# Cross attention scores: the low-key products of two neighbouring tiles as two 64-row products in the two halves of the array

## The chip, the cores and the metric

The kernel runs on one core of one Trainium2 chip. A core has TensorE (PE) for matmuls, VectorE (DVE), ScalarE (ACT) and GpSimd (POOL) for the rest, and SyncE (SP), which here issues the DMAs. Each engine takes its instructions in order and waits on semaphores. The metric is the device time of one execution in microseconds (us). Before the change three runs took 3082.76, 3084.55 and 3085.52 us; the median is 3084.55.

## The reference

A perceiver-like network of 6 layers on 4 batches, then a small attention and a gated recurrence over the batches. Per layer and batch: causal self attention over 128 rows, cross attention of 128 rows over a context of 2048 rows, and a gated feed-forward part. All are 16 heads of width 64 with one key/value head that the heads share. What the change touches is the score product of the cross attention:

```python
q = (xn @ wq).reshape(b, n, H, DH).transpose(0, 2, 1, 3) * SCALE      # 16 heads x 128 rows
k, v = jnp.split(kv @ wkv, 2, axis=-1)                                # kv is the context, 2048 rows
nk, nv = null_kv                                                      # one more key and value
k = jnp.concatenate((nk, k), axis=1)
q = l2norm(q) * math.sqrt(SCALE)
k = l2norm(k) * math.sqrt(SCALE)
sim = jnp.einsum('bhid,bjd->bhij', q, k)
attn = jax.nn.softmax(sim, axis=-1)
out = jnp.einsum('bhij,bjd->bhid', attn, v)
```

## The kernel before

**Precision.** Queries and keys are each split into a high and a low fp16 half of width 64 (high = the fp16 rounding, low = the rest). `QT[:, par]` holds the turned queries: high in partitions 0 to 63, low in 64 to 127, 2048 columns (16 heads x 128 rows). `KT[:, par, part]` holds the turned keys twice: part 0 is high over low, part 1 low over high. A tile's score is two full 128-row matmuls, part 0 and part 1, into one PSUM bank (`scores`, line 936), which gives all four products of halves. The probabilities are split too: `PH` is the rounded exponential, `P` the full one (both ACT, lines 786 and 789), `PL = P - PH` (DVE, line 549), and the value product is three matmuls, V with PH, VL with PH and V with PL (lines 985, 986, 988).

**Rounds and steps.** There are 24 runs (6 layers x 4 batches). Each has 64 tiles (4 groups of 4 heads x 16 tiles of 128 keys). The function `drive` writes, for every engine, windows of 65 steps. In a window the tiles ("core") of run n stand beside the front of run n+1 (self attention, projections, keys and queries of the cross attention) and the back of run n-1 (output, feed-forward). Step 0 is the scores of the null key, step s from 1 the tile s-1. After the core's step come the stages that a table names for this step: PLAN_PE, PLAN_ACT, PLAN_DVE and PLAN_POOL. An engine never leaves this order. Names with f_ belong to the front, with b_ to the back, with e_ to the core.

**A step of PE.** Scores of tile s-1 into bank `s % 3` of psS, and the value sums of the tile of step s-AHEAD (AHEAD = 6). Before it writes the bank, step s waits until ACT has finished with the tile of step s-3, `pe.wait_ge(sem("ca_exp"), n * TILES + s - SLOTS)`. ACT takes a step's two exponentials, then its stages; DVE in step s takes the subtraction of step s-1. P has 4 slots, PH and PL 8.

**Stages that matter here.** On PE: f_proj_sa (step 5) projects the self attention's queries; f_turn_q_sa (15) turns them; f_sk1 (25) gives self attention scores, which ACT's f_se1 (23 of ACT's table) takes; f_sv1 and b_up stand at 31, f_sk2 at 32, f_sk3 at 37, f_sv3 at 43, f_wo at 48; f_proj_ca and f_turn_k0 at 53, f_turn_k1 at 56, f_turn_q_ca at 62. f_turn_k0 and f_turn_k1 turn the keys, 16 transposes each, which ACT (line 868) and DVE (line 610) copy into KT. ACT's f_QT_ca (line 804) copies the queries into QT, after which the next round's step 0 may begin.

Of the kernel before, what the change touches and what calls it, by code (L numbers as in the profile page):

```python
# [36 lines left out]
AHEAD = 6  # L37
# [25 lines left out]
def build(nc, x, ctxT, wpack, gcols, gout, null_k, null_v, tail_w, tail_cols, bo, emb,  # L63
          c_pack, out):
    with ExitStack() as ctx:
# [89 lines left out]
        ks = sb("ks", [128, KT_N, 3, DH], F16)  # L155
        KT = sb("KT", [128, 2, 2, M], F16)
# [23 lines left out]
        PL = sb("PL", [128, HSLOTS, QCOL], F32R)  # L180
# [43 lines left out]
        def at(s, core, back):  # L224
# [17 lines left out]
            31: ["f_se2"], 36: ["f_se3"], 52: ["f_raw_ca"], 53: ["f_KT0", "f_sq_ca"], 56: ["f_KT1"], 58: ["f_hi_ca"],  # L242
# [40 lines left out]
        def _(sp):  # L283
# [37 lines left out]

            for n in range(1, B):
                context(n)
            with sp.Fori(1, L) as l:
                context(l * B)
                sp.wait_ge(sem("ca_proj"), l * B * 2)
                front_weights(l)
                context(l * B + 1)
                sp.wait_ge(sem("ff_w2"), l * B)
                back_weights(l)  # L330
                context(l * B + 2)
                context(l * B + 3)
            sp.wait_ge(sem("ca_proj"), RUNS * 2)
# [9 lines left out]
        def _(pool):  # L343
# [40 lines left out]
            def low(tag, half, whole, high):  # L384
# [10 lines left out]
                "f_klow": low("kv", ks[:, :, 1, :], kn[:], ks[:, :, 0, :]),  # L395
# [13 lines left out]
        def _(dve):  # L409
# [130 lines left out]
            def core_step(s, core, back):  # L540

                step = at(s - LOW, core, back)
                if step is None or step[0] == 0:
                    return
                t, n, par = step[0] - 1, step[1], step[2]
                dve.wait_ge(sem("p_hi"), n * TILES + t + 1)
                dve.wait_ge(sem("ca_exp"), n * TILES + t + 1)
                here = t % HSLOTS
                nc_v.tensor_tensor(PL[:, here, :], P[:, t % PSLOTS, :], PH[:, here, :], ALU.subtract).then_inc(sem("p_lo"), 1)  # L549
# [210 lines left out]
        def _(act):  # L760
# [98 lines left out]
            def f_khi(n, par):  # L859
                act.wait_ge(sem("kv_kn"), n + 1)  # L860
                for a in (0, 2):
# [3 lines left out]
            def f_KT(part):  # L865
                def stage(n, par):
                    act.wait_ge(sem("kv_T"), n * 4 + 2 * part + 1)
                    nc_a.activation(KT[:, par, part, 0:1024], psLh[0].rearrange("p t c -> p (t c)"), ACT.Copy).then_inc(sem("kv_KT_a"), 1)
                return stage
# [13 lines left out]
            for part in range(2):  # L883
                stages[f"f_KT{part}"] = f_KT(part)
# [23 lines left out]
        def _(pe):  # L908
# [40 lines left out]
            def core_step(s, core, back):  # L949

                if core is not None:
                    n, par = core
                    first = isinstance(n, int) and n == 0
                    if s == 0:
                        pe.wait_ge(sem("ca_QT"), n * 2 + 2)
                        pe.wait_ge(sem("kv_KT_a"), n * 2 + 2)
# [4 lines left out]
                    if s == SLOTS:  # L961
                        pe.wait_ge(sem("ca_nexp"), n + 1)
                    elif s > SLOTS:
                        pe.wait_ge(sem("ca_exp"), n * TILES + s - SLOTS)
                    elif not first:
                        pe.wait_ge(sem("ca_exp"), n * TILES - (STEPS - 1 - max(t for t in range(STEPS - SLOTS, STEPS) if t % SLOTS == s)))
                    bank = psS[:, s % SLOTS, :]
                    if s == 0:
                        null_scores(bank, [nkc[:, par, p, :] for p in range(2)], QT[:, par], True).then_inc(sem("ca_nqk"), 1)
                    else:  # L970
                        g, j = (s - 1) // KT_N, (s - 1) % KT_N
                        scores(bank, [KT[:, par, p, 128 * j:128 * j + 128] for p in range(2)], QT[:, par, g * QCOL:(g + 1) * QCOL]).then_inc(sem("ca_qk"), 1)
# [15 lines left out]
                mm(bank, V[:, par, j, :], PL[:, here, :], start=False, stop=(j == KT_N - 1)).then_inc(sem("ca_pv"), 1)  # L988
# [81 lines left out]
            def f_turn_q_ca(n, par):  # L1070
                pe.wait_ge(sem("kv_KT_a"), n * 2 + 2)
# [3 lines left out]
            def f_turn_k(part):  # L1075
                def stage(n, par):
                    pe.wait_ge(sem("kv_lo"), n + 1)
                    for i in range(2):
                        if part == 1:
                            pe.wait_ge(sem("kv_KT_a" if i == 0 else "kv_KT_v"), n * 2 + 1)  # L1080
                        else:
                            pe.wait_ge(sem("ca_raw"), n * 2 + i + 1)
                        for t in range(8):
                            ins = nc.tensor.transpose(psLh[i][:, t, :], ks[:, 8 * i + t, part:part + 2, :].rearrange("p a d -> p (a d)"), ident16[:])
                        ins.then_inc(sem("kv_T"), 1)
                return stage
# [33 lines left out]
            for part in range(2):  # L1120
                stages[f"f_turn_k{part}"] = f_turn_k(part)
# [138 lines left out]
```

## Time and profile before

| | |
|---|---|
| median of 3 runs | 3084.55 us |
| profiled execution: its own time / its span | 3083.15 us / 3081.4 us |
| PE busy (matmuls) | 2670.2 us, 87% of the span |
| DVE busy | 2352.4 us, 76% |
| ACT busy | 2115.6 us, 69% |
| POOL busy | 606.1 us, 20% |
| mean granted TensorE clock | 0.944 of full speed |
| scores of the tiles (line 939) | 3072 matmuls |
| value sums (lines 985, 986, 988) | 1536 matmuls each |

The span is from the first to the last instruction. Matmuls overlap, and each one's duration in the profile is its way through the array; how fast PE really goes is read from start to start. An engine's idle time is put down to the engine and line that ended it last.

### The profile page before, as it was taken

The numbers are of one execution on the slowest core, as the hardware profiler recorded it, in microseconds if no ns is written. First come the engines' busy times: TensorE is split into PE (matmuls) and PEld (weight loads), VectorE is DVE, ScalarE is ACT, GpSimd is POOL, SyncE is SP. The second block draws the span as 40 slices with busy tenths as digits, with TensorE's granted clock in tenths as the row PEclk, the third lists the DMA queues.
The fourth block names the chain that finished last, engine by engine and source line by source line (L and its number), as shares of the span: only waits on it lengthen the run. The fifth ranks groups of instructions, "written<-read, shape, count | busy, mean of one in ns | idle before, by whom it ended". The sixth has DMA issues, their size and how long they took to land.

```text
span 3081.4 us, 44915 instructions
## 1 busy us (share of the span) xinstructions
PE 2670.2 (87%) x13036; PEld 1575.0 (51%) x13036; DVE 2352.4 (76%) x4396; ACT 2115.6 (69%) x3898; POOL 606.1 (20%) x392
## 2 busy tenths in 40 slices
PE   3698988998998988989989999898899989989856
PEld 1355545555554555555555555555455555555535
DVE  4587877877777877877788787787778778787665
ACT  2487777777777767768678677777777777677601
POOL 2212212212212213113113023022122122120000
PEclk8799999999999999999999999999999999999866
DMA  3000000000000000001001001001001001000000
GB/s 109 14 1 15 15 24 15 1 32 16 15 24 15 1 32 15 1 14 38 1 1 47 1 14 38 1 1 47 1 14 39 1 1 47 1 1 12 1 1 4
DMA packets 11436, 51.72 MB, mean 17 GB/s; under 512 B 1361, under 2 KB 6018, under 8 KB 6410
## 3 DMA queue, kind: packets, MB, share of 16 engines
q1 hardware_dynamic: 11146, 48.28, 4.5%
q8 instruction: 129, 2.11, 0.3%
q14 instruction: 161, 1.32, 0.1%
HBM read 47.99 MB, written 0.29 MB: 16 GB/s over the span
## 4 chain that ended last, share of the span: by engine, by line
PE 49%; DVE 18%; issue 16%; ACT 10%; POOL 5%; DVEq 1%; DMA 0%; ACTq 0%; SPq 0%; POOLq 0%
PE psS L939 13%; PE psO L985 7%; PE psO L986 6%; PE psO L988 6%; ACT P L789 5%; DVE PL L549 5%; ACT PH L786 3%; POOL rn L353 3%; PE psL L1031 3%; PE psL L939 2%; PE psL L1042 2%; PE psL L1049 1%; DVE rows_sb L528 1%; PE psL L1032 1%; DVE oTs L533 1%
## 5 line engine op out<-in xcount | busy, mean ns | idle before, releaser
L549 DVE TENSOR_TENSOR PL<-P,PH 128x512 fp32r<-128x512 f32 x1536 | 1168.1, 785 | 129.4 <-ACT P L789 83.6
L786 ACT ACTIVATE PH<-psS 128x512 fp32r<-128x512 f32 x1536 | 944.5, 615 | 250.8 <-PE psS L939 227.2
L939 PE MATMUL psS<-QT,KT 128*128 128x512 f16 x3072 | 949.8, 393 | 14.8 <-ACT P L789 12.4
L789 ACT ACTIVATE P<-psS 128x512 f32<-128x512 f32 x1536 | 949.7, 618 | 18.8 <-DVE PL L549 16.2
L985 PE MATMUL psO<-PH,V 128*128 128x512 f32 x1536 | 902.8, 588 | 0.0
L986 PE MATMUL psO<-PH,VL 128*64 128x512 f32 x1536 | 614.9, 400 | 0.0
L988 PE MATMUL psO<-PL,V 128*128 128x512 f32 x1536 | 613.7, 400 | 0.0
L985 PEld LDWEIGHTS psO<-PH,V 128*128 128x128 f32 x1536 | 299.7, 195 | 208.3 <-issue 33.7
L939 PEld LDWEIGHTS psS<-QT,KT 128*128 128x128 f16 x3072 | 219.0, 100 | 354.0 <-issue 232.3
L988 PEld LDWEIGHTS psO<-PL,V 128*128 128x128 f32 x1536 | 295.0, 192 | 152.3 <-issue 8.1
L353 POOL TENSOR_TENSOR front_rstd<-front_ve,neghalf 128x1 f32<-128x1 f32 x84 | 45.5, 542 | 1491.9 <-DVE front_ve L417 1491.9
L353 POOL TENSOR_TENSOR rn<-ssc,neghalf 128x16 f32<-128x16 f32 (+2 forms) x73 | 235.0, 3220 | 359.8 <-DVE ssc L484 306.2
L837 ACT ACTIVATE Ps<-psL 128x512 f32<-128x512 f32 x96 | 57.7, 601 | 288.1 <-PE psL L939 288.1
L986 PEld LDWEIGHTS psO<-PH,VL 128*64 128x64 f32 x1536 | 215.3, 140 | 40.4
L939 PE MATMUL psL<-QTs,KTs 128*128 128x512 f16 x192 | 67.9, 441 | 101.4 <-DVE oTs L533 99.2
L388 POOL TENSOR_TENSOR qs_all<-qsq,qs_all 128x1088 f16<-128x1088 f32 (+1 forms) x48 | 116.4, 2426 | 139.3 <-ACT qs_all L796 139.3
L528 DVE STREAM_TRANSPOSE rows_sb<-rcol 64x512 f32<-64x512 f32 x192 | 135.8, 707 | 5.2
L932 PE MATMUL psL<-ident,qs_all 128*128 128x128 f16 x768 | 55.8, 230 | 87.2 <-POOL qs_all L388 61.0
L578 DVE TENSOR_TENSOR Ps<-Ps,ET 128x512 f32<-128x512 f32 x96 | 66.0, 688 | 73.1 <-ACT Ps L837 73.1
L808 ACT ACTIVATE qraw<-psL 128x512 f32<-128x512 f32 x96 | 57.3, 597 | 82.7 <-PE psL L1049 62.2
L1061 PEld LDWEIGHTS psL<-W,ctx_sb 128*128 128x128 f32 x768 | 99.0, 192 | 26.0 <-ACT qraw L808 14.4
L1061 PE MATMUL psL<-W,ctx_sb 128*128 128x128 f32 x768 | 104.0, 279 | 3.5 <-ACT kraw L851 3.5
(310 smaller groups left out, 2947.7 us busy)
## 6 DMA issues: line engine op xcount, KB each, us to landing
ctx_sb<-ctxT SPq DMA_DIRECT2D x24, 1024.0 KB, 4.8
W<-wpack SPq DMA_DIRECT2D x6, 1664.0 KB, 6.3
W<-wpack SPq DMA_DIRECT2D x6, 1280.0 KB, 5.6
ctx_sb<-biasM SPq DMA_DIRECT2D x1, 1024.0 KB
W<-tail_w SPq DMA_DIRECT2D x1, 832.0 KB
kraw<-biasW SPq DMA_DIRECT2D x1, 512.0 KB
ksq<-biasW SPq DMA_DIRECT2D x1, 512.0 KB
P<-null_v SPq DMA_DIRECT2D x1, 384.0 KB
```

The source lines that it names most:

```text
L353: nc.gpsimd.tensor_tensor(out_, in_, neghalf[0:out_.shape[0], 0:width], ALU.pow).then_inc(sem(done), 1)
L388: nc.gpsimd.tensor_tensor(half, whole, high, ALU.subtract).then_inc(sem(tag + "_lo"), 1)
L528: nc_v.transpose(rr, rc.unsqueeze(2).broadcast_to([64, QCOL // 32, 32])).then_inc(sem(tag + "_row"), 1)
L549: nc_v.tensor_tensor(PL[:, here, :], P[:, t % PSLOTS, :], PH[:, here, :], ALU.subtract).then_inc(sem("p_lo"), 1)
L786: nc_a.activation(PH[:, t % HSLOTS, :], bank, ACT.Exp, scale=SIM_SCALE).then_inc(sem("p_hi"), 1)
L789: nc_a.activation(P[:, t % PSLOTS, :], bank, ACT.Exp, scale=SIM_SCALE).then_inc(sem("ca_exp"), 1)
L939: ins = mm(bank, keys[part], q, start=(part == 0), stop=(part == 1))
L985: mm(bank, V[:, par, j, :], PH[:, here, :], start=False, stop=False)
L986: mm(bank[0:DH, :], VL[:, par, j, :], PH[:, here, :], start=False, stop=False)
L988: mm(bank, V[:, par, j, :], PL[:, here, :], start=False, stop=(j == KT_N - 1)).then_inc(sem("ca_pv"), 1)
L1031: mm(psL[:, g % 2, :], Vs[:], Ps[:, g % 2, :], start=True, stop=False)
L1061: ins = mm(psL[:, t % 2, a * 128:(a + 1) * 128], ctx_sb[:, k * 128:(k + 1) * 128], weights(W_CAKV, W_CAKV + 128), start=True, stop=True)
```

## The change

The scores of a tile become one full product and one half product. KT now holds the high keys twice, so that one full matmul gives high keys times high and low queries. The low keys stand in KL: those of even tiles in partitions 0 to 63, those of odd tiles in 64 to 127, and are multiplied with the high queries only. For odd tiles the high queries must stand in partitions 64 to 127 too; SP copies them there by a DMA of 64 x 2048 fp16 values (QB). At an odd step PE issues the half products of this tile and of the next, into two banks, and then this tile's full product; at an even step only the full product. The product of low keys and low queries is no longer computed. Keys now need 24 transposes instead of 32, and one ACT copy less. PL shrinks from 8 to 4 slots, with a wait of DVE for the value sum of the tile four back, and AHEAD goes from 6 to 5.

```diff
-AHEAD = 6
+LSLOTS = 4
+AHEAD = 5
...
-        ks = sb("ks", [128, KT_N, 3, DH], F16)
-        KT = sb("KT", [128, 2, 2, M], F16)
+        ks = sb("ks", [128, KT_N, 2, DH], F16)
+        kl = sb("kl", [128, KT_N // 2, 2, DH], F16)
+        KT = sb("KT", [128, 2, M], F16)
+        KL = sb("KL", [128, 2, M // 2], F16)
+        QB = sb("QB", [128, 2, H * N], F16)
...
-            31: ["f_se2"], 36: ["f_se3"], 52: ["f_raw_ca"], 53: ["f_KT0", "f_sq_ca"], 56: ["f_KT1"], 58: ["f_hi_ca"],
+            31: ["f_se2"], 36: ["f_se3"], 52: ["f_raw_ca"], 53: ["f_KT0", "f_sq_ca"], 58: ["f_hi_ca"],
...
+            def queries_below(n, par):
+                sp.wait_ge(sem("ca_QT"), n * 2 + 2)
+                sp.dma_start(QB[64:128, par, :], QT[0:64, par, :]).then_inc(sem("ca_QB"), 16)
...
+                if t >= LSLOTS or not isinstance(n, int) or n > 0:
+                    dve.wait_ge(sem("ca_pv"), n * TILES + t - LSLOTS + 1)
+                nc_v.tensor_tensor(PL[:, t % LSLOTS, :], P[:, t % PSLOTS, :], PH[:, here, :], ALU.subtract).then_inc(sem("p_lo"), 1)
...
-                    dve.wait_ge(sem("kv_T"), n * 4 + 2 * part + 2)
-                    ins = nc_v.tensor_copy(KT[:, par, part, 1024:2048], psLh[1].rearrange("p t c -> p (t c)"))
-                    ins.then_inc(sem("kv_KT_v"), 1)
+                    dve.wait_ge(sem("kv_T"), n * 3 + 2 + part)
+                    dst = KL[:, par, :] if part else KT[:, par, 1024:2048]
+                    nc_v.tensor_copy(dst, psLh[1 - part].rearrange("p t c -> p (t c)")).then_inc(sem("kv_KT_v"), 1)
...
-                    elif s > SLOTS:
-                        pe.wait_ge(sem("ca_exp"), n * TILES + s - SLOTS)
...
-                        scores(bank, [KT[:, par, p, 128 * j:128 * j + 128] for p in range(2)], QT[:, par, g * QCOL:(g + 1) * QCOL]).then_inc(sem("ca_qk"), 1)
+                        t = s - 1
+                        g, j = t // KT_N, t % KT_N
+                        cols = slice(g * QCOL, (g + 1) * QCOL)
+                        if t % 2 == 0:
+                            if s == 1:
+                                pe.wait_ge(sem("ca_QB"), n * 16 + 16)
+                            if s == SLOTS:
+                                pe.wait_ge(sem("ca_nexp"), n + 1)
+                            if s >= SLOTS or not first:
+                                pe.wait_ge(sem("ca_exp"), n * TILES + max(0, s + 1 - SLOTS))
+                            pair = slice(64 * j, 64 * j + 128)
+                            mm(bank, KL[0:64, par, pair], QT[0:64, par, cols], start=True, stop=False)
+                            mm(psS[:, (s + 1) % SLOTS, :], KL[64:128, par, pair], QB[64:128, par, cols], start=True, stop=False)
+                        mm(bank, KT[:, par, 128 * j:128 * j + 128], QT[:, par, cols], start=False, stop=True).then_inc(sem("ca_qk"), 1)
...
+            def f_turn_k1(n, par):
+                pe.wait_ge(sem("kv_KT_a"), n + 1)
+                for t in range(8):
+                    ins = nc.tensor.transpose(psLh[0][:, t, :], kl[:, t].rearrange("p a d -> p (a d)"), ident16[:])
+                ins.then_inc(sem("kv_T"), 1)
```

The order on PE at steps 25 and 26, before. The names are output<-inputs, ca_exp counts the tiles that ACT is done with, psL<-QTs,KTs is the self attention score f_sk1:

```order
L939 MATMUL psS<-QT,KT 128x512 [waits ca_exp]
L939 MATMUL psS<-QT,KT 128x512
L985 MATMUL psO<-PH,V 128x512 [waits p_hi]
L986 MATMUL psO<-PH,VL 64x512
L988 MATMUL psO<-PL,V 128x512 [waits p_lo]
L939 MATMUL psL<-QTs,KTs 128x512 [waits sa_nexp,sa_KT,sa_QT]
L939 MATMUL psL<-QTs,KTs 128x512
L964 REGISTER_ALU
L939 MATMUL psS<-QT,KT 128x512 [waits ca_exp]
```

The same place of the changed kernel:

```order
L992 MATMUL psS<-QT,KL 128x512 [waits ca_exp]
L993 MATMUL psS<-QB,KL 128x512
L994 MATMUL psS<-QT,KT 128x512
L1006 REGISTER_ALU
L1007 MATMUL psO<-PH,V 128x512 [waits p_hi]
L1008 MATMUL psO<-PH,VL 64x512
L1010 MATMUL psO<-PL,V 128x512 [waits p_lo]
L953 MATMUL psL<-QTs,KTs 128x512 [waits sa_nexp,sa_KT,sa_QT]
L953 MATMUL psL<-QTs,KTs 128x512
L994 MATMUL psS<-QT,KT 128x512
```

The odd step now has three score matmuls, two of them with 64 rows, and carries the only wait for ca_exp of the pair; the even step has one matmul and no such wait.

The DMA issues of SP in the loop over layers, before (ISA and REGISTER_ALU rows only compute addresses and counts):

```order
L320 DMA ctx_sb<-ctxT 128x2048 [waits kv_proj]
L326 REGISTER_ALU
L290 ISA [waits ca_proj]
L290 DMA W<-wpack 128x3328
L291 ISA
L291 DMA gsa<-gout 128x128
L319 ISA
L320 DMA ctx_sb<-ctxT 128x2048 [waits kv_proj]
```

And changed:

```order
L324 DMA ctx_sb<-ctxT 128x2048 [waits kv_proj]
L336 REGISTER_ALU
L294 ISA [waits ca_proj]
L294 DMA W<-wpack 128x3328
L295 ISA
L295 DMA gsa<-gout 128x128
L328 ISA
L329 DMA QB<-QT 64x2048 [waits ca_QT]
L323 ISA
L324 DMA ctx_sb<-ctxT 128x2048 [waits kv_proj]
```

The copy QB stands behind the context of the next run and, once in four runs, behind the weights of the next layer, in SP's one queue; the following context stands behind QB.

## Rows read from the trace of the kernel before

**Rows 1.** Page, section 1 and section 5: busy time by engine; a group of instructions.
```profile
PE 2670.2 (87%) x13036; PEld 1575.0 (51%) x13036; DVE 2352.4 (76%) x4396; ACT 2115.6 (69%) x3898; POOL 606.1 (20%) x392
...
L549 DVE TENSOR_TENSOR PL<-P,PH 128x512 fp32r<-128x512 f32 x1536 | 1168.1, 785 | 129.4 <-ACT P L789 83.6
```
**Rows 2.** Timeline of PE, a bare step: start us, us, engine, line, operation.
```profile
1528.18 0.61 PE L939 MATMUL psS<-QT,KT 128*128 128x512 f16 x2
...
1529.10 0.39 PE L988 MATMUL psO<-PL,V 128*128 128x512 f32 x1
1529.33 0.60 PE L939 MATMUL psS<-QT,KT 128*128 128x512 f16 x2
```
**Rows 3.** Timeline of PE around matmuls of another shape (rows*columns of the array).
```profile
1564.51 0.39 PE L988 MATMUL psO<-PL,V 128*128 128x512 f32 x1
1564.83 0.62 PE L946 MATMUL psL<-QTs,nkcs 128*32 128x512 f16 x8
1565.38 0.49 PE L1025 MATMUL psL<-B,group_rows 8*128 8x512 f32 x1
1565.80 0.60 PE L939 MATMUL psS<-QT,KT 128*128 128x512 f16 x2
```
**Rows 4.** Timeline of PE: scores of step 25, f_sk1, scores of step 27.
```profile
1570.28 0.60 PE L939 MATMUL psS<-QT,KT 128*128 128x512 f16 x2
...
1571.42 0.60 PE L939 MATMUL psL<-QTs,KTs 128*128 128x512 f16 x2
...
1573.69 0.60 PE L939 MATMUL psS<-QT,KT 128*128 128x512 f16 x2 [0.54 <-ACT P L789]
```
**Rows 5.** Timeline of ACT: P of step 23, f_se1, P of steps 24 and 25.
```profile
1570.32 0.61 ACT L789 ACTIVATE P<-psS 128x512 f32<-128x512 f32 x1
1572.06 0.60 ACT L837 ACTIVATE Ps<-psL 128x512 f32<-128x512 f32 x1 [1.13 <-PE psL L939]
...
1573.03 0.60 ACT L789 ACTIVATE P<-psS 128x512 f32<-128x512 f32 x1
...
1573.98 0.63 ACT L789 ACTIVATE P<-psS 128x512 f32<-128x512 f32 x1
```
**Rows 6.** Timelines of PE and ACT: scores of step 39, P of step 37.
```profile
1599.63 0.60 PE L939 MATMUL psS<-QT,KT 128*128 128x512 f16 x2
...
1599.67 0.60 ACT L789 ACTIVATE P<-psS 128x512 f32<-128x512 f32 x1
```
**Rows 7.** Waits of the whole execution: us in total, times, longest us.
```profile
PE psL L939 <- DVE oTs L533: 99.2, 22, 4.5
PE psL L932 <- POOL qs_all L388: 61.0, 25, 7.9
...
PE psS L939 <- ACT P L789: 12.4, 23, 0.5
...
DVE hu L629 <- PE psA L1097: 108.3, 24, 4.7
```
**Rows 8.** Timelines of PE and ACT at a round's end: transposes, QT, null scores, step 1.
```profile
1521.70 1.05 PE L932 MATMUL psL<-ident,qs_all 128*128 128x128 f16 x16 [1.14 <-DVE KT L610]
...
1522.72 1.94 ACT L804 ACTIVATE QT<-psL 128x1024 f16<-128x1024 f16 x2
...
1525.69 0.61 PE L946 MATMUL psS<-QT,nkc 128*32 128x512 f16 x8 [0.66 <-ACT P L789]
...
1527.03 0.61 PE L939 MATMUL psS<-QT,KT 128*128 128x512 f16 x2
```
**Rows 9.** Timeline of ACT: the second key copy and the high query halves.
```profile
1513.44 1.13 ACT L868 ACTIVATE KT<-psL 128x1024 f16<-128x1024 f16 x1
...
1517.17 1.06 ACT L796 ACTIVATE qs_all<-qsq 128x1024 f16<-128x1024 f32 x1 [0.64 <-DVE qsq L491]
```
**Rows 10.** DMA issues: how many, KB each, median us from issue to landing.
```profile
ctx_sb<-ctxT SPq DMA_DIRECT2D x24, 1024.0 KB, 4.8
...
out<-x_in SPq DMA_DIRECT2D x4, 64.0 KB, 1.5
```

More of the change, by code:

```diff
@@ L179, in build @@
         PH = sb("PH", [128, HSLOTS, QCOL], F32R)
[L180 removed]
+        PL = sb("PL", [128, LSLOTS, QCOL], F32R)
         Pn = sb("Pn", [128, QCOL], F32R)
@@ L860, in f_khi, with f_KT0 @@
                 act.wait_ge(sem("kv_kn"), n + 1)
-                for a in (0, 2):
+                for a in range(2):
                     ins = nc_a.activation(ks[:, :, a, :], kn[:], ACT.Copy)
                 ins.then_inc(sem("kv_hi"), 1)
[L865 to L869, printed above, removed]
+            def f_KT0(n, par):
+                act.wait_ge(sem("kv_T"), n * 3 + 1)
+                nc_a.activation(KT[:, par, 0:1024], psLh[0].rearrange("p t c -> p (t c)"), ACT.Copy).then_inc(sem("kv_KT_a"), 1)
             def b_tanh(n, par):
@@ L882, in _ @@
                 stages[f"f_kraw{g}"] = f_kraw(g)
-            for part in range(2):
-                stages[f"f_KT{part}"] = f_KT(part)
+            stages["f_KT0"] = f_KT0
             drive(act, PLAN_ACT, stages, core_step)
@@ L959, in core_step @@
                         pe.wait_ge(sem("kv_v"), n * 4 + 4)
-                    if s == SLOTS:
-                        pe.wait_ge(sem("ca_nexp"), n + 1)
-                    elif s > SLOTS:
-                        pe.wait_ge(sem("ca_exp"), n * TILES + s - SLOTS)
-                    elif not first:
-                        pe.wait_ge(sem("ca_exp"), n * TILES - (STEPS - 1 - max(t for t in range(STEPS - SLOTS, STEPS) if t % SLOTS == s)))
                     bank = psS[:, s % SLOTS, :]
                     if s == 0:
+                        if not first:
+                            pe.wait_ge(sem("ca_exp"), n * TILES - 1)
                         null_scores(bank, [nkc[:, par, p, :] for p in range(2)], QT[:, par], True).then_inc(sem("ca_nqk"), 1)
                     else:
-                        g, j = (s - 1) // KT_N, (s - 1) % KT_N
-                        scores(bank, [KT[:, par, p, 128 * j:128 * j + 128] for p in range(2)], QT[:, par, g * QCOL:(g + 1) * QCOL]).then_inc(sem("ca_qk"), 1)
+                        t = s - 1
[12 more added lines that the diff above has]
+                        mm(bank, KT[:, par, 128 * j:128 * j + 128], QT[:, par, cols], start=False, stop=True).then_inc(sem("ca_qk"), 1)
                 step = at(s - AHEAD, core, back)
@@ L987, in core_step @@
                 pe.wait_ge(sem("p_lo"), n * TILES + t + 1)
-                mm(bank, V[:, par, j, :], PL[:, here, :], start=False, stop=(j == KT_N - 1)).then_inc(sem("ca_pv"), 1)
+                mm(bank, V[:, par, j, :], PL[:, t % LSLOTS, :], start=False, stop=(j == KT_N - 1)).then_inc(sem("ca_pv"), 1)
             def weights(a, b):
@@ L1070, in f_turn_q_ca, with f_turn_k0 @@
             def f_turn_q_ca(n, par):
-                pe.wait_ge(sem("kv_KT_a"), n * 2 + 2)
+                pe.wait_ge(sem("kv_KT_a"), n + 1)
                 pe.wait_ge(sem("kv_KT_v"), n * 2 + 2)
                 turn_q("ca")(n, par)
[L1075 to L1086, printed above, removed]
+            def f_turn_k0(n, par):
+                pe.wait_ge(sem("kv_lo"), n + 1)
+                for i in range(2):
+                    pe.wait_ge(sem("ca_raw"), n * 2 + i + 1)
+                    for t in range(8):
+                        ins = nc.tensor.transpose(psLh[i][:, t, :], ks[:, 8 * i + t].rearrange("p a d -> p (a d)"), ident16[:])
+                    ins.then_inc(sem("kv_T"), 1)
+            def f_turn_k1(n, par):
+                pe.wait_ge(sem("kv_KT_a"), n + 1)
+                for t in range(8):
+                    ins = nc.tensor.transpose(psLh[0][:, t, :], kl[:, t].rearrange("p a d -> p (a d)"), ident16[:])
+                ins.then_inc(sem("kv_T"), 1)
             def b_gate(n, par):
@@ L1119, in _ @@
                 stages[f"f_kv{g}"] = f_kv(g)
-            for part in range(2):
-                stages[f"f_turn_k{part}"] = f_turn_k(part)
+            stages["f_turn_k0"], stages["f_turn_k1"] = f_turn_k0, f_turn_k1
             drive(pe, PLAN_PE, stages, core_step)
```

10 lines of the change are left out of this document (7 added, 3 removed).

## The prediction

> **What bounds the kernel now.** I read the page first: PE is busy 87% of the span, ACT 69%, DVE 76% [rows 1]. One profiled execution took 3083.15 us, of which the span is 3081.4; the median of the runs is 1.4 us above it. The work repeats in rounds of about 117.8 us, one per batch and layer: 64 score tiles in 64 steps, and between them the stages of the next round's front and the last one's back. 24 rounds have tiles, 23 of them beside a front. I number steps as the code does, step 0 being the null scores.
>
> The timeline of PE shows a bare step: from one pair of score matmuls to the next 1.15 us, for five passes of 512 columns, so 0.23 each [rows 2]. ACT, when it has a backlog, needs 0.95 us for a tile's two exponentials (from 1573.03 to 1573.98 in [rows 5]). So in bare steps PE is the limit and ACT has 0.2 us to spare, out of which it must pay its front stages (0.6 to 2 us each) in clumps.
>
> The waits show where neither counts. PE waits for the query halves at step 15 (POOL's qs_all, 61.0 us in 25 times), at step 32 for the scaled self attention (oTs, 99.2 us in 22 times, up to 4.5), both in [rows 7], and at step 62 for the key copy (1.14 us in [rows 8]). These end chains over ACT, POOL and DVE that a PE stage started: the projection at step 5, the "up" product at step 31 (DVE itself waited 108.3 us for it), the second value product at step 43, the cross projection at step 53. Whatever PE saves between the start and the end of such a chain becomes a longer wait. The end of the round is one chain from step 53 to step 0: after the transposes (step 62) comes QT on ACT, then two tiles, and only then do the null scores start [rows 8].
>
> **The score passes.** Before, two full matmuls for each tile; now an odd step has two half-array ones, meant to run side by side (one pass), and a full one, an even step one full one. Free of other cost that saves one pass of 0.23 us in each even step. But the array changes its shape before and after the halves. The nearest rows: a full matmul to the 32-column null scores took 0.32 us instead of 0.23; the eight of these took 0.55 to the next, two passes (0.46) and 0.09; and the 8-row matmul to the next full one 0.42, which is 0.19 above a pass, with an exposed fp32 weight load in it [rows 3]. So a change of shape costs 0.09 to 0.19 us; I take 0.09, the two f16 cases, since KL, KT and nkc are all f16. Odd step: 1.15 + 2 x 0.09 = 1.33, that is +0.18. Even step: 1.15 - 0.23 = 0.92, that is -0.23. A pair gains 0.05 us, and since chains start at odd steps (5, 25, 31, 37, 43, 53), a stretch often has one odd step more.
> The Trainium skill, "TensorEngine Tiling (Array Packing)", Key Properties, says that changing the tiling mode drains the array, which speaks against this change; [rows 3] agree with 0.09. By its table Theoretical Speedup alone (up to 2x for 64 rows) the whole pass would be gained; that is the first rival below. That two row halves start within some 4 ns is in "TensorE: Matmul & The Clock Gate", The mechanism; no row here shows row halves, the four column groups of [rows 3] behave so.
>
> **The tighter wait, the main term.** Step s used to wait for the exponentials of step s-3. An odd step now opens two banks at once and waits for step s-2; an even step waits for none. Queued behind this wait are all of PE's matmuls of the step and the stages after it. Where ACT works off a clump this is late:
> - Step 25: PE began it at 1570.28 [rows 4]; the exponentials of step 23 ended at 1570.32 + 0.61 = 1570.93 [rows 5]. Late by 0.65.
> - Step 27: began at 1573.69 after 0.54 of waiting for step 24 [rows 4]; step 25's end at 1573.98 + 0.63 = 1574.61, late by 0.92. It doesn't merge with the first: between them ACT waited 1.13 us for the self attention score that PE issues behind step 25 [rows 5], so both add.
> - Step 39: began at 1599.63, step 37's end at 1600.27: late by 0.64 [rows 6].
> - Elsewhere (steps 7 and 61) it is late too, but inside the chains 5 to 15 and 53 to 0, which have the room; at other odd steps it is early by 0.5 and more in bare stretches.
>
> **Smaller parts.** (a) QB: 256 KB moved by DMA once QT is done. QT ends at 1522.72 + 1.94 = 1524.66, step 1 begins at 1527.03 [rows 8], so 2.4 us are free. 64 KB landed in 1.5 us, 1024 KB in 4.8 [rows 10]; a line through both gives 2.2 for 256 KB. I take 0.1 us of stall; bounds nothing and 2.4 us (4.8 less 2.4) a round. SP issues it behind a context load and weights that were released long before step 62. (b) Eight transposes and one ACT copy of 1.1 us fewer per round. The copy stood at 1513.44, and ACT then waited anyway until 1517.17 for DVE's unit queries [rows 9]: nothing gained. The transposes go inside the same chain: nothing. If both lay on the path: 1.1 + 0.5 us a round. (c) PL has 4 slots, so DVE waits for the sum four tiles back; with the sums one step earlier (AHEAD 5) that sum is issued in the same step, where DVE comes later than PE in nearly all steps: nothing, bound 0.8 us a round (the mean length of one such DVE operation [rows 1]). The last sums end one step earlier: -1 us once. The low-times-low product that is dropped costs and saves nothing by itself.
>
> **The sum for a round.** Steps 1 to 5: 3 x 0.18 - 2 x 0.23 = +0.1, with QB +0.2. Steps 5 to 15: hidden. Steps 16 to 22, until ACT's clump begins: 3 x 0.18 - 4 x 0.23 = -0.4. Step 25: +0.65 - 0.35 = +0.3. Step 27: + 0.09 + 0.92 = +1.3. To step 31: +0.0. The chain to step 32 keeps its length. Steps 33 to 37 +0.1, step 39 +0.6. 39 to 43: 0. 43 to 48 hidden. 49 to 53: +0.1. 53 to 0 hidden. In all 0.2 + 1.3 + 0.7 + 0.1 = 2.3 us. Times 23: +53. The last round has no front: 32 pairs x -0.05 = -1.6. With the -1 at the end: +50. 3083.15 + 50 + 1.4 = **3135 us** by the median.
>
> **Rivals.**
> 1. The change of shape is hidden (halves are loaded while the array drains). Odd steps +0, even -0.23: stretch 1 to 5 -0.4, the clump at 25 is met early, 27 leaves +0.5, 33 to 39 +0.2, 39 to 43 -0.5, 49 to 53 -0.5: -0.6 a round, -14 us, 3070; with the transposes and the copy on the path too (1.6 x 23 = 37) 3034. For: nothing in [rows 3]. It decides below about 0.04 us a change. Chance 0.21, faster.
> 2. The waits at 25, 27 and 39 don't add up to 2.2 but to the one at 27, since ACT starts its clump earlier: 2.3 - 1.3 - 0.6 = +0.4, less the transposes: within 0.2%, 3086. Chance 0.10.
> 3. The halves run one after the other. Each of about 16 odd steps outside the chains pays 0.23 more: 3.7 x 23 = +85, 3220. Against: the column groups of [rows 3] overlap. Likewise with changes of 0.19 (0.2 more in as many): 3205. Chance 0.14.
> 4. QB lands 2.4 us late in each round: +55, 3190. Chance 0.06.
> The forecast has 0.49. Results within 0.2% (6 us) can't be told from no change. Faster 0.21 (rival 1), same 0.10, slower 0.69. The range from 3060 to 3215 leaves out the far end of rivals 1 and 3; the forecast's own is 3105 to 3170.
>
> **What would show it.** In the changed profile: the half matmuls of a pair start within 0.01 us of each other, and the full one 0.3 us later, not 0.23; bare pairs take 2.25 us, not 2.30. PE's waits for ACT's P before the scores, 12.4 us in all before [rows 7], come to 50 or more, in groups at steps 25, 27 and 39, while the waits for qs_all and oTs grow a little. DMA QB lands in 2 to 2.5 us and PE hardly waits for it. ACT's busy time falls by some 26 us (24 copies), to no effect. It is wrong if a bare pair takes 2.1 us or less, or if a round comes out at or below 117.8 us.

## The result, and the profile after

The changed kernel takes 3185.2 us (median of 4 runs, 3183.88 to 3188.49), the kernel before beside it 3085.0. The ratio is 1.0328, 95% interval 1.0310 to 1.0346: slower by 100 us. The prediction said slower by 50. The time lies inside its whole range (3060 to 3215), but outside the 3105 to 3170 that it gave for its own mechanism.

The profiled execution of the changed kernel took 3188.49 us, its span 3186.7. Busy time by engine, and the group of the subtraction P - PH on DVE, against [rows 1]:

```profile
PE 2686.3 (84%) x12844; PEld 1495.6 (47%) x12844; DVE 2341.8 (73%) x4396; ACT 2075.3 (65%) x3874; POOL 611.3 (19%) x392
...
L566 DVE TENSOR_TENSOR PL<-P,PH 128x512 fp32r<-128x512 f32 x1536 | 1156.7, 774 | 267.9 <-PE psO L1010 218.1
```

ACT has 40 us less work, and PE 192 instructions fewer (with 16 us more busy time, since some of them run at the lower clock), and both only idle more. The bare steps came out nearly as forecast. Timeline of PE after (start us, us, engine, line), one pair of bare steps, against [rows 2]:

```profile
1684.67 0.39 PE L992 MATMUL psS<-QT,KL 64*128 64x512 f16 x1
1684.68 0.39 PE L993 MATMUL psS<-QB,KL 64*128 64x512 f16 x1
1685.00 0.39 PE L994 MATMUL psS<-QT,KT 128*128 128x512 f16 x1
...
1685.92 0.39 PE L994 MATMUL psS<-QT,KT 128*128 128x512 f16 x1
...
1686.62 0.39 PE L1010 MATMUL psO<-PL,V 128*128 128x512 f32 x1
1686.94 0.39 PE L992 MATMUL psS<-QT,KL 64*128 64x512 f16 x1
```

The two halves start 0.01 us apart, the full product 0.32 behind them, and at 1686.94 the next halves 0.32 behind a full one, instead of 0.23: two changes of shape of 0.09 each. The pair takes 2.27 us (1684.67 to 1686.94), against two bare steps of 1.15 before, so the two changes of shape eat nearly all of the pass that the halves save. The Trainium skill, "TensorEngine Tiling (Array Packing)", Key Properties, says that a change of the tiling mode drains the array; the trace agrees, with 0.09 us for each.

The waits of the whole execution (us in total, times, longest), against [rows 7]:

```profile
PE psS L992 <- ACT P L806: 110.2, 78, 2.0
PE psL L953 <- DVE oTs L548: 103.7, 22, 4.7
PE psL L946 <- POOL qs_all L403: 55.9, 25, 9.4
...
PE psO L1010 <- DVE PL L566: 13.5, 22, 0.6
...
PE psS L992 <- DMA QB<-QT: 9.5, 15, 1.9
```

The first was 12.4 us before and has grown most. The timelines of one round show steps 25 and 27, against [rows 4, 5]. PE:

```profile
1621.22 0.40 PE L1010 MATMUL psO<-PL,V 128*128 128x512 f32 x1
1622.37 0.39 PE L992 MATMUL psS<-QT,KL 64*128 64x512 f16 x1 [0.76 <-ACT P L806]
...
1624.74 0.39 PE L1010 MATMUL psO<-PL,V 128*128 128x512 f32 x1
1626.86 0.39 PE L992 MATMUL psS<-QT,KL 64*128 64x512 f16 x1 [1.73 <-ACT P L806]
```

ACT at the same time:

```profile
1621.71 0.60 ACT L806 ACTIVATE P<-psS 128x512 f32<-128x512 f32 x1
1624.25 0.60 ACT L854 ACTIVATE Ps<-psL 128x512 f32<-128x512 f32 x1 [1.94 <-PE psL L953]
...
1626.18 0.63 ACT L806 ACTIVATE P<-psS 128x512 f32<-128x512 f32 x1
```

Step 25 starts when P of step 23 is done (1621.71 + 0.60), 0.76 late, and step 27 when P of step 25 is done (1626.18 + 0.63), 1.73 late where it was 0.54 before. Between the two ACT waits 1.94 us for the self attention scores that PE issues behind step 25: the waits do add up. Step 39, against [rows 6]:

```profile
1653.29 0.50 PE L1005 MATMUL psO<-Pn,nv 32*128 32x512 f32 x1
...
1654.29 0.40 PE L1010 MATMUL psO<-PL,V 128*128 128x512 f32 x1
1654.82 0.39 PE L992 MATMUL psS<-QT,KL 64*128 64x512 f16 x1
```

Here the gap is 1654.82 less 1654.29, 0.53, of which 0.32 is usual: 0.2 late, not 0.64. With AHEAD 5 the null value's matmul (L1005), one step earlier than before, stands in step 38 and fills the rest.

The end of the round went otherwise than forecast. Timelines at steps 60 to 62, against [rows 8, 9]. PE:

```profile
1688.88 0.39 PE L1010 MATMUL psO<-PL,V 128*128 128x512 f32 x1
1691.28 0.39 PE L992 MATMUL psS<-QT,KL 64*128 64x512 f16 x1 [2.01 <-ACT P L806]
...
1692.53 0.60 PE L994 MATMUL psS<-QT,KT 128*128 128x512 f16 x1
...
1693.35 0.63 PE L1008 MATMUL psO<-PH,VL 128*64 128x512 f32 x1
1693.78 0.63 PE L1010 MATMUL psO<-PL,V 128*128 128x512 f32 x1
1694.21 1.93 PE L946 MATMUL psL<-ident,qs_all 128*128 128x128 f16 x16
```

ACT there:

```profile
1689.20 1.06 ACT L813 ACTIVATE qs_all<-qsq 128x1024 f16<-128x1024 f32 x1 [1.68 <-DVE qsq L506]
...
1690.64 0.59 ACT L806 ACTIVATE P<-psS 128x512 f32<-128x512 f32 x1
1691.12 0.60 ACT L803 ACTIVATE PH<-psS 128x512 fp32r<-128x512 f32 x1
```

ACT stands in f_hi_ca 1.68 us for DVE, then computes qs_all, and only then P of step 59, for which step 61 now waits: 2.01 us. After that the matmuls start 0.43 apart instead of 0.23 (1693.35 to 1693.78), and the 16 transposes take 1.93 instead of 1.05. The clock tells why. Windows of that place (stretch: length, busy us of PE, PEld, DVE, ACT, POOL, then the granted clock):

```profile
1688.90:1691.20 2.30, 0.38 (x2) 0.00 (x0) 2.17 (x6) 2.00 (x4) 0.87 (x1) 1.00 0.00 0
1691.30:1692.50 1.20, 1.20 (x6) 0.61 (x6) 1.20 (x1) 1.20 (x3) 1.16 (x1) 1.00 0.00 0
1692.60:1695.90 3.30, 3.30 (x21) 2.47 (x20) 3.30 (x6) 2.35 (x5) 0.00 (x0) 0.50 0.02 5
```

PE idled for most of 2.3 us, ran 1.2 us at 2.4 GHz and then 3.3 us at 1.2 GHz. In steps 60 to 64 this happened in 16 of 23 rounds, 54.6 us at the lower level in all, and in none before. The mean clock is 0.934, before it was 0.944.

The lengths by stretch. A round of the tiles takes 117.9 us before and 122.1 after (from a run's first score product to the next run's, mean over rounds 4 to 21, the first being 0), +4.2; the 23 rounds together are 97 us longer. The table has the cumulated difference to the kernel before, in us a round, up to the first score product of a step, and beside it the forecast's own sum. It goes by odd steps: an odd step now holds three of the pair's four score products, so that an even step starts later by construction:

| up to step | 25 | 27 | 31 | 37 | 43 | 53 | 59 | next round |
|---|---|---|---|---|---|---|---|---|
| forecast | +0.5 | +1.5 | +1.5 | +1.6 | +2.2 | +2.3 | +2.3 | +2.3 |
| changed kernel | +1.1 | +2.2 | +2.2 | +2.7 | +2.8 | +2.9 | +2.5 | +4.2 |

### The profile page after: what moved, and what is told of

The parts are those of the page before. It is cut to its first block, busy times and chain, and to the rows that moved or that the text cites. A ratio compares the mean times of both kernels' runs of the same rounds, so it can differ in the third digit from the quotient of the medians.

```text
span 3186.7 us, 44651 instructions
## 1 busy us (share of the span) xinstructions
PE 2686.3 (84%) x12844; PEld 1495.6 (47%) x12844; DVE 2341.8 (73%) x4396; ACT 2075.3 (65%) x3874; POOL 611.3 (19%) x392
## 4 chain that ended last, share of the span: by engine, by line
PE 64%; issue 9%; ACT 9%; DVE 9%; POOL 5%; DMA 2%; DVEq 1%; ACTq 0%; SPq 0%; POOLq 0%
PE psS L994 11%; PE psO L1007 9%; PE psO L1010 9%; PE psO L1008 9%; PE psS L992 7%; POOL rn L368 3%; ACT P L806 3%; PE psL L1053 3%; ACT PH L803 2%; POOL qs_all L403 2%; PE psL L953 2%; PE psL L1064 2%; DMA QB<-QT 1%; PE psL L1071 1%; PE psL L1083 1%
## 5 line engine op out<-in xcount | busy, mean ns | idle before, releaser
L1010 PE MATMUL psO<-PL,V 128*128 128x512 f32 x1536 | 622.2, 405 | 13.5 <-DVE PL L566 13.5
L994 PE MATMUL psS<-QT,KT 128*128 128x512 f16 x1536 | 612.8, 399 | 0.0
L992 PE MATMUL psS<-QT,KL 64*128 64x512 f16 x768 | 305.3, 397 | 122.8 <-ACT P L806 110.2
L1007 PEld LDWEIGHTS psO<-PH,V 128*128 128x128 f32 x1536 | 313.8, 204 | 40.1 <-issue 27.8
L994 PEld LDWEIGHTS psS<-QT,KT 128*128 128x128 f16 x1536 | 149.8, 98 | 341.3 <-issue 333.2
L993 PE MATMUL psS<-QB,KL 64*128 64x512 f16 x768 | 305.3, 397 | 0.0
L992 PEld LDWEIGHTS psS<-QT,KL 64*128 64x128 f16 x768 | 71.3, 93 | 376.6 <-ACT P L806 237.8
```

The costliest lines, as they stand in the source:

```text
L992: mm(bank, KL[0:64, par, pair], QT[0:64, par, cols], start=True, stop=False)
L993: mm(psS[:, (s + 1) % SLOTS, :], KL[64:128, par, pair], QB[64:128, par, cols], start=True, stop=False)
L994: mm(bank, KT[:, par, 128 * j:128 * j + 128], QT[:, par, cols], start=False, stop=True).then_inc(sem("ca_qk"), 1)
L1007: mm(bank, V[:, par, j, :], PH[:, here, :], start=False, stop=False)
L1010: mm(bank, V[:, par, j, :], PL[:, t % LSLOTS, :], start=False, stop=(j == KT_N - 1)).then_inc(sem("ca_pv"), 1)
```

## Experiments

Each was timed beside the kernel before (3081.9, 3083.2, 3085.4 and 3085.0 us in four groups). A difference is to the kernel before of the same group; two kernels of different groups are compared by these differences. "A round" is measured as above. "Half clock" is time at the lower of the two levels of the granted clock, 1.2 GHz instead of 2.4; it is summed over the 23 rounds of the profiled execution.

**1. The wait alone.** The old order of passes, the tighter wait.

```diff
-                        pe.wait_ge(sem("ca_exp"), n * TILES + s - SLOTS)
+                        pe.wait_ge(sem("ca_exp"), n * TILES + s - SLOTS + s % 2)
```

> The kernel before, with one change: odd steps wait for the exponentials of step s-2 instead of s-3. No half products, no QB, AHEAD 6. Theory A (the tighter wait, and the half clock that PE falls into behind the longer waits, are the loss): slower by 60 to 110 us, PE's wait for ACT P before the scores above 80 us in all, a gap of about 2 us at step 61. Rival B (the changes of the array's shape and the longer odd steps are the loss): at most 15 us slower.

3127.5 us, ratio 1.0143 (1.0126 to 1.0160), +46. PE waits 95.2 us in 118 times for P before the scores. Up to step 43 a round is 2.3 us longer, but 0.7 comes back at step 48 (a shorter wait of f_wo), and the 1.4 at step 61 comes back by step 63. The loss lies between what the two theories gave, nearer to A: the wait alone costs nearly half of the 100 us. The gap at step 61 is 1.2 us, not the 2 that A named, and no half clock follows it; in all the rounds have 94 us of half clock, fewer than the 155 before.

**2. Pair order with full products.** The changed kernel's order, its wait, but 128-row low products, no KL, no QB.

```diff
+                        if t % 2 == 0:
+                            ...
+                            for i in range(2):
+                                mm(psS[:, (s + i) % SLOTS, :], KT[:, par, 1, 128 * (j + i):128 * (j + i) + 128], QT[:, par, cols], start=True, stop=False)
+                        mm(bank, KT[:, par, 0, 128 * j:128 * j + 128], QT[:, par, cols], start=False, stop=True).then_inc(sem("ca_qk"), 1)
```

> The kernel before, but an odd step opens both banks with the two low-over-high products as full 128-row matmuls and then its own high-over-low one; an even step has one matmul. Same wait as the changed kernel, no change of shape, no QB, AHEAD 6. A pair of bare steps should take 2.29 us. Theory A: within 15 us of the changed kernel (3170 to 3200). Rival B: clearly faster than that, 3100 or less.

3160.9 us, ratio 1.0253 (1.0236 to 1.0270), +79, again between the theories and near A: most of the loss without a single half product. Over experiment 1 it adds 1.8 us a round, 0.7 of it between steps 31 and 37, where 6.1 us a round instead of 3.8 run at half clock behind the wait for oTs. The rest comes in smaller pieces, most of them after step 53.

**3. PL and AHEAD.** The kernel before with AHEAD 5, 4 slots of PL and DVE's wait; and with AHEAD 5 only.

```diff
-AHEAD = 6
+LSLOTS = 4
+AHEAD = 5
...
+                if t >= LSLOTS or not isinstance(n, int) or n > 0:
+                    dve.wait_ge(sem("ca_pv"), n * TILES + t - LSLOTS + 1)
```

> The kernel before with AHEAD 5, PL in 4 slots and DVE's wait for the value sum four tiles back, nothing else. Both theories, as the prediction had it: within 5 us of before. Rival C (the 218 us for which DVE waits for PE's value sums in the changed kernel delay the stages behind them): slower by 20 us or more.

> The kernel before with AHEAD 5 and nothing else, PL in 8 slots without DVE's wait. Theory A: as slow as with both edits (3115 to 3130). Rival C: within 5 us of before.

Both: 3125.3 us, 1.0142 (1.0126 to 1.0159), +43: rival C of the first holds, and "nothing" was wrong for this part by itself. AHEAD 5 only: 3102.2 us, 1.0065 (1.0048 to 1.0082), +19: here neither theory came true, for AHEAD and the slots have about half each. Timeline of PE at step 19 with both:

```profile
1573.44 0.40 PE L989 MATMUL psO<-PH,VL 128*64 128x512 f32 x1
1574.66 0.50 PE L991 MATMUL psO<-PL,V 128*128 128x512 f32 x1 [0.82 <-DVE PL L552]
```

DVE is behind with its front stages, and with the sum one step earlier PE waits 0.82 us for PL, where it had a step in hand before.

**4. All but the halves.** Experiments 2 and 3 together: the change without KL, QB and the fewer transposes.

> The kernel before with everything of the change except the halves: pair order and its wait with full 128-row low products, AHEAD 5 and 4 PL slots; no KL, no QB, all 32 key transposes and the ACT copy kept. Theory A (the halves are worth 0.04 us in an odd step, and eight transposes fewer 0.5 us a round): 0.6 + 0.5 us a round more than the changed kernel, 3200 to 3215 us. Theory B (the halves save a good part of a pass after all and the change's other parts hide it): 3225 or more. Theory C (the halves cost more than the passes they save, or QB does): at or below 3180.

3160.4 us, ratio 1.0242 (1.0225 to 1.0259), +75. Two findings. AHEAD 5 and PL add nothing to pair order (+79 without them): at step 23 this kernel is 0.7 us a round behind experiment 2, at step 25, behind the wait for P, only 0.1. And the changed kernel is 25 us slower than this one, so the halves, with QB and with fewer transposes and one copy less, did not gain a little but lost, as theory C said.

**5. Where the halves lose: the clock at steps 61 to 64.** Three edits of the changed kernel at the end of the round: eight unused matmuls in PE's wait at step 60; f_hi_ca one step later on ACT; the eight transposes of the low keys twice, so that PE has as many as before.

```diff
-            56: ["f_turn_k1"], 62: ["f_turn_q_ca"],
+            56: ["f_turn_k1"], 60: ["f_warm"], 62: ["f_turn_q_ca"],
...
+                for _ in range(8):
+                    mm(psL[:, 1, :], QTs[:, 0:128], QTs[:, 0:512], start=True, stop=True)
```
```diff
-            31: ["f_se2"], 36: ["f_se3"], 52: ["f_raw_ca"], 53: ["f_KT0", "f_sq_ca"], 58: ["f_hi_ca"],
+            31: ["f_se2"], 36: ["f_se3"], 52: ["f_raw_ca"], 53: ["f_KT0", "f_sq_ca"], 59: ["f_hi_ca"],
```
```diff
-                for t in range(8):
+                for t in [*range(8), *range(8)]:
                     ins = nc.tensor.transpose(psLh[0][:, t, :], kl[:, t].rearrange("p a d -> p (a d)"), ident16[:])
```

> The changed kernel with eight unused 128x512 fp16 matmuls (1.8 us) into an idle bank after step 60, in front of the 2.0 us wait of step 61. They only fill the wait. Theory A1 (the clock falls to half in that wait, which makes the rest of step 61, step 62 and the query transposes slow): 15 to 35 us faster than the changed kernel, transposes of step 62 in 1.05 us instead of 1.9. Rival (the lost time there is ACT's and DVE's chain alone): within 5 us of the changed kernel, or up to 10 slower.

> The changed kernel with ACT's f_hi_ca one step later, at 59, so that the exponentials of step 59, for which PE's step 61 waits, are done in ACT's 1.7 us of idling and not behind it. Theory A: the gap of 2.0 us at step 61 goes, the clock stays up at step 62, 20 to 35 us faster than the changed kernel. Rival (step 62 is bound by the chain over hi and POOL in any case): within 5 us.

> The changed kernel with the eight transposes of the low keys at step 56 issued twice over the same bank (the second pass gives the same result), so that TensorE does as many as before, 32 a round. Theory A (the eight transposes saved are worth less than nothing: PE comes to step 61 earlier, waits 2.0 us instead of 1.3 there, and its clock is halved in steps 61 to 64, 1.0 us a round): 15 to 25 us below the changed kernel. Theory B (the half clock there has another cause, the halves themselves): eight transposes more cost nothing or 12 us, 3183 to 3197.

| | us | ratio (95%) | us at half clock in steps 60 to 64, rounds | a round |
|---|---|---|---|---|
| changed kernel | 3185.2 | 1.0328 (1.0310 to 1.0346) | 54.6 in 16 | +4.2 |
| unused matmuls | 3161.9 | 1.0263 (1.0246 to 1.0280) | 0 | +3.2 |
| f_hi_ca at 59 | 3167.4 | 1.0273 (1.0256 to 1.0290) | 22.5 in 11 | +3.2 |
| transposes twice | 3162.3 | 1.0249 (1.0232 to 1.0266) | 0 | +3.2 |
| experiment 4 | 3160.4 | 1.0242 (1.0225 to 1.0259) | 0 | +3.2 |

Against the kernel before these are +80, +84 and +77, where the changed kernel has +100. More work on PE makes it faster, and the round is then as long as that of experiment 4. That bears the clock out: the first and the third came as theory A said. With f_hi_ca at 59 the wait at step 61 is gone, but it gained 16 instead of 20 to 35: in 11 rounds the half clock came later, 22.5 us up to step 64 and 15.0 more before the next round. The same place with the transposes twice, timeline of PE:

```profile
1682.60 0.39 PE L992 MATMUL psS<-QT,KL 64*128 64x512 f16 x1 [1.57 <-ACT P L806]
...
1683.85 0.39 PE L994 MATMUL psS<-QT,KT 128*128 128x512 f16 x1
...
1685.03 1.05 PE L946 MATMUL psL<-ident,qs_all 128*128 128x128 f16 x16
```

And windows of its wait and of what follows:

```profile
1680.70:1682.60 1.90, 0.34 (x2) 0.00 (x1) 1.77 (x5) 1.90 (x4) 0.95 (x1) 1.00 0.00 0
1682.70:1686.00 3.30, 3.21 (x26) 1.97 (x24) 3.30 (x4) 2.83 (x6) 1.08 (x1) 1.00 0.00 0
```

The wait is 1.57 instead of 2.01, the clock stays at 1.00, and the transposes take 1.05 again. So what the saved transposes gave (0.44 us a round between steps 53 and 59) became idle time before step 61, and with that idle time came the half clock. Experiment 4, with ACT's second key copy and the full products as well, takes another 0.3 us from step 53 to step 59 and then waits less still (timeline of PE at step 61):

```profile
1678.71 0.60 PE L979 MATMUL psS<-QT,KT 128*128 128x512 f16 x2 [1.25 <-ACT P L792]
```

Where the repairs take off their 1.0 us a round: with the clock up, steps 61 to 63 take 3.4 us instead of 4.4. Half of that is lost again before the next round starts; the other half comes with the first steps of the next round (in the changed kernel step 3 waits for P in five rounds in which it doesn't here) and with less half clock in steps 31 to 37.

One caution. The mean rounds of seven kernels (experiments 2 and 4, these three, and the two of experiment 6) lie between 121.16 and 121.20 us, though at step 53 they stand up to 0.5 apart. What draws them together was not found. So equal rounds do not show equal costs, and a part of a few tenths of a us a round can't be read from them.

**6. QB.** Its first 512 columns in a DMA of their own, as soon as the first half of QT is done, the rest behind it, for which PE waits only at step 17; then the same with the transposes twice.

```diff
-                sp.wait_ge(sem("ca_QT"), n * 2 + 2)
-                sp.dma_start(QB[64:128, par, :], QT[0:64, par, :]).then_inc(sem("ca_QB"), 16)
+                sp.wait_ge(sem("ca_QT"), n * 2 + 1)
+                sp.dma_start(QB[64:128, par, 0:512], QT[0:64, par, 0:512]).then_inc(sem("ca_QB"), 16)
+                sp.wait_ge(sem("ca_QT"), n * 2 + 2)
+                sp.wait_ge(sem("ca_QB"), n * 32 + 16)
+                sp.dma_start(QB[64:128, par, 512:], QT[0:64, par, 512:]).then_inc(sem("ca_QB"), 16)
```

> The changed kernel with QB copied by two DMAs, 512 of its 2048 columns as soon as the first half of QT is done, the rest behind it, waited for at step 17. Theory A (PE's waits for QB at step 1, 9.5 us in 15 times, and the later step 1 are the 0.3 us a round that the changed kernel is behind at step 2 against the same order without halves): 5 to 9 us below the changed kernel. Theory B (the wait is covered by the null scores' exponentials in the same steps): within 3 us of it.

> Both edits together, transposes twice and QB in two DMAs. Theory A (these two places are the whole 25 us by which the changed kernel is slower than the same order with full low products): 3155 to 3165 us. Theory B (the halves cost in the bare steps too): 3175 or more.

3158.8 us, 1.0237 (1.0220 to 1.0254), and with the transposes twice 3159.0, 1.0240 (1.0223 to 1.0257). The wait for QB is gone from PE's waits. The first gained 26 us, not 5 to 9, and the second nothing on top; it ends where theory A had it, but not by adding two gains. The surplus goes with the clock: half clock in the rounds fell from 198 us to 131, in two places. In steps 60 to 64, with step 61's wait unchanged, it fell from 54.6 us in 16 rounds to 10.2 in 3, and the stretch from step 53 to the next round is 0.6 us shorter; in steps 31 to 37, which the edit doesn't touch, from 126 us to 82, and they are 0.7 shorter. One of the three rounds, timeline of PE:

```profile
1679.11 0.61 PE L997 MATMUL psS<-QT,KL 64*128 64x512 f16 x1 [2.01 <-ACT P L809]
```

Windows of the wait and of what follows:

```profile
1676.80:1679.10 2.30, 0.30 (x2) 0.00 (x0) 2.17 (x6) 2.08 (x4) 0.94 (x1) 0.99 0.00 0
1679.20:1682.40 3.20, 3.20 (x9) 1.66 (x10) 3.20 (x4) 2.37 (x5) 1.08 (x1) 0.50 0.00 0
```

The same wait of 2.01 us, yet here the clock is down at once, not 1.2 us later, and in 20 other rounds with the same wait not at all. The wait's length alone does not decide it; what else does was not found. QB's wait by itself (9.5 us in all) was therefore not priced cleanly.

**7. AHEAD 6 with 4 slots.** The changed kernel with AHEAD 6 again.

> The changed kernel with AHEAD back at 6 (PL keeps its 4 slots, since 8 don't fit beside QB). Theory A (the value sums one step earlier meet DVE's late subtraction of tile 13 at step 19, and the half clock follows): 20 to 45 us faster than the changed kernel, PE's wait for PL gone. Rival C (PL in 4 slots is what costs): no faster than the changed kernel, rather slower, since DVE must now wait one step longer.

3339.0 us, ratio 1.0832 (1.0814 to 1.0850), 156 slower than the changed kernel: theory C. Waits of DVE over the whole execution:

```profile
DVE PL L566 <- PE psO L1010: 549.5, 393, 6.5
```

And of PE:

```profile
PE psS L992 <- ACT P L806: 165.2, 120, 3.4
```

With 4 slots and the sum six steps behind, DVE waits for the sum before it may write PL, and ACT and PE wait in turn. AHEAD 5 belongs to the 4 slots. The changed kernel with AHEAD 6 and 8 slots was not tried.

**8. The chain at step 32.** [rows 7] show 99.2 us of PE waiting for oTs and 108.3 of DVE waiting for the up product. b_up moved from step 31 to 28, in the kernel before; the same in the changed kernel, and there with the unused matmuls; and in the kernel before with f_hi_ca at 59.

```diff
-            23: ["f_sk0"], 25: ["f_sk1"], 27: ["f_sv0"], 31: ["f_sv1", "b_up"], 32: ["f_sk2"], 37: ["f_sv2", "f_sk3"],
+            23: ["f_sk0"], 25: ["f_sk1"], 27: ["f_sv0"], 28: ["b_up"], 31: ["f_sv1"], 32: ["f_sk2"], 37: ["f_sv2", "f_sk3"],
```

> The kernel before with one stage moved: b_up on PE from step 31 to step 28, where DVE's b_act already waits for it. Theory (DVE's 108 us of waiting for b_up and PE's 99 us for oTs are one chain that b_up starts): the wait at step 32 shrinks from 4.5 to about 1.5 us, round shorter by 2 to 3.5 us, 50 to 80 us faster. Rival (the wait at step 32 comes from elsewhere, DVE's own queue): within 10 us of before.

> The changed kernel with one stage moved: the up product (b_up) from step 31 to step 28 on TensorE, which took 141 us from the kernel before. Theory A (the change's loss lies in its wait, in AHEAD with four PL slots and at step 61, none of them in the chain from the up product to step 32): the same gain, 3030 to 3060 us, so that about 100 us between the two kernels stay. Theory B (the late step 27 and the up product stand side by side, so the chain starts later than with the old wait): half the gain, 3100 to 3130. Theory C (part of the loss was a longer step 32 wait): more gain than before, below 3020.

> The changed kernel with the up product at step 28 and eight unused matmuls at step 60, which took 23 us from it. Theory A (the two repairs are independent): 20 to 25 us below the changed kernel with the up product moved alone. Theory B (with the shorter round the wait at step 61 is there no more): within 5 us of it or slower.

> The kernel before with the up product at step 28 and ACT's f_hi_ca one step later (59 instead of 58), which took 18 us from the changed kernel. Theory A (the move helps only where the tighter wait makes step 61 wait for ACT): within 5 us of the kernel with the up product moved alone, 2937 to 2947. Theory B (ACT's clump before step 61 costs the kernel before too): 2920 to 2932. Theory C (it delays QT and the next round): above 2950.

| b_up at 28 in | us | ratio (95%) |
|---|---|---|
| the kernel before | 2941.9 | 0.9545 (0.9529 to 0.9561) |
| the same, f_hi_ca at 59 | 2945.9 | 0.9542 (0.9526 to 0.9558) |
| the changed kernel | 3046.2 | 0.9872 (0.9856 to 0.9889) |
| the same, unused matmuls | 3041.9 | 0.9847 (0.9827 to 0.9866) |

The first is the fastest kernel of the study and beats both. Both theories had put the gain lower. Timeline of DVE at that place in the kernel before:

```profile
1583.32 0.69 DVE L629 SCALAR_TENSOR_TENSOR hu<-psA,eg 128x512 f32<-128x512 f32 x1 [4.66 <-PE psA L1097]
1584.05 0.72 DVE L520 STREAM_TRANSPOSE rows_sb<-psL 64x512 f32<-64x512 f32 x1
...
1587.99 0.42 DVE L533 TENSOR_TENSOR oTs<-psL,rows_sb 64x256 f32<-64x256 f32 x1
```

With b_up at 28:

```profile
1500.20 1.29 DVE L549 TENSOR_TENSOR PL<-P,PH 128x512 fp32r<-128x512 f32 x2
1501.41 0.68 DVE L629 SCALAR_TENSOR_TENSOR hu<-psA,eg 128x512 f32<-128x512 f32 x1
1502.13 0.72 DVE L520 STREAM_TRANSPOSE rows_sb<-psL 64x512 f32<-64x512 f32 x1
```

DVE stood 4.66 us in front of hu, and the steps to oTs, for which PE waits at step 32, are queued behind it. Moved, that wait is gone, and with it the half clock behind it (102 us in 22 rounds in steps 32 to 37, none now). The round is 6.8 us shorter. The changed kernel gains 139 us by the same edit, and 102 stay between the two: its loss lies outside this chain (theory A). In the kernel before f_hi_ca at 59 changes nothing (theory A). The unused matmuls gain nothing that can be told there (-4 us, single runs from 3032 to 3049; theory B): without them only 5 rounds have half clock in steps 60 to 64, though the wait at step 61 is still 2.0 us in every round, not gone as theory B had it.

## Why the prediction was right in direction and half the size

- **Change of shape, 0.09 each:** right. With both changes counted in the odd step it takes 1.34, the even one 0.93, the pair 2.27 (forecast 2.25). The halves gain next to nothing: experiment 4, without them, is as fast as the repaired versions (+75 against +77 to +84).
- **Waits at 25 and 27:** right, and they add. Step 25 is late by 0.7 in experiment 1 (forecast 0.65), and from step 25 to 27 the changed kernel loses 1.1 (forecast 1.0). The credit of 0.35 for a PE that comes early to step 25 did not come: the wait there ends when ACT ends.
- **Step 39:** the wait is there (+0.7 in experiment 1), but AHEAD 5 hides most of it. Oversized by 0.4.
- **Steps 7 and 61 "inside the chains 5 to 15 and 53 to 0, which have the room":** right for 7, and this is the step that failed for 61. The room was read from [rows 8]: PE waited 1.14 us at step 62 for the key copy. The new wait at step 61 is 2.0 us. From step 53 to the next round the change adds 1.3 us where the forecast had nothing, times 23 is 30 of the missing 50 us. With the clock kept up it is still 0.8 to 0.9 (experiment 5), so the wait is more than the room even then; the wait of 1.2 us in experiment 1 fitted in and cost nothing, while in experiments 2 and 4, with about the same one, the stretch is 0.5 us longer.
- **The clock:** the second thing that failed, since the prediction had no term for it. A wait was priced at its length, but its end can bring 3.3 us at 1.2 GHz, which cost 1.0 us a round on average between steps 61 and 63. Keeping the clock up there is worth the 16 to 23 us of experiment 5. Of the difference between experiments 1 and 2, 0.7 of 1.8 us a round lies where half clock grew.
- **The transposes, "nothing":** worse than nothing. They shorten steps 53 to 59 by 0.44 us, and all of it becomes wait before step 61.
- **The rest of the missing 50:** 0.6 us a round, 14 us in all, are there by step 53, and the profiled execution is 8 us longer outside the rounds, where the forecast had it 2.6 shorter (it is itself 3 us above the median); that part was not looked into.
- **(c) PL and AHEAD, "nothing, bound 0.8 us a round":** wrong as a price by itself (+43 us, 1.5 a round), right for the sum only because the waits for P cover it (experiment 4), which the prediction did not say: that is luck. The reason given, that DVE comes later than PE, speaks of the write side; it was PE that then waited for DVE at step 19.
- **Signs:** the wait for oTs grew by 4.5 us as said, that for qs_all fell by 5.1. ACT lost 40 us of work instead of 26, without effect as said.
- **(a) QB:** landed in 3.1 us, not 2.2 (row below), and PE waited 9.5 us in 15 times, 0.4 a round for a forecast of 0.1.

```profile
QB<-QT SPq DMA_DIRECT2D x24, 256.0 KB, 3.1
```

- **Rivals.** Rival 1 fell with the 0.32 after each change, rival 2 with the separate waits at 25 and 27, rival 3 with halves that start together and changes of 0.09, rival 4 with 0.4 us of wait instead of 2.4. Two of their sums are slightly off as written (rival 1's terms add to -0.7, not -0.6 a round, and changes of 0.19 give 3209, not 3205), to no effect.

The direction and about half of the size rest on a right mechanism, the tighter wait; the other half does not. That 3185 still lies inside the whole range is owed to the room left for rivals 3 and 4, both of which fell. The parts, each added to the ones before it: wait +46, pair order +33, AHEAD 5 and PL -4 (none that can be told), halves with copies, transposes and QB +25; together the 100. None of them is its waits alone: half clock in the rounds is 155 us before, 94 with the wait, 141 with pair order, 122 in experiment 4 and 198 in the changed kernel. Open is why the clock falls in one round and not in another that has the same wait. Half open is AHEAD 5 alone: the profiled execution is 12 us longer, of which 7 lie in the rounds, and the median is 7 us above that execution.

## What to carry to other kernels

A saved pass is worth something only where the engine is not about to wait; in front of a wait it becomes idle time, which can cost the clock on top. Price a tighter wait at every place where the consumer is behind, also inside a chain, and compare it with the wait at that chain's end: a new wait of 2.0 us did not fit where that one was 1.14. And look first for an engine that stands before one late input with a chain queued behind it: here it was DVE before the up product, and starting that input three steps earlier was worth 141 us, more than the whole change cost.

## What was not expected of the hardware

- After a wait of 2.0 us TensorE ran some 3.3 us at 1.2 GHz (0.43 us from matmul to matmul instead of 0.23), sometimes at once and sometimes only after 1.2 us of full work: in 16 of 23 rounds of the changed kernel, in 3 of 23 with QB in two DMAs, with the same wait in each. After waits of 1.57, 1.25 and 1.21 us at that place it never did. Eight matmuls whose result nobody reads, or eight repeated transposes, took 20 and 23 us off a kernel of 3185.
- A copy of 256 KB within SBUF, 64 partitions to 64 others, landed in 3.1 us (2.8 to 3.6), while one of 1024 KB from memory landed in 4.8 [rows 10].
